# Storing and reloading kept blocks in halves, with later reload positions, in a two-channel convolution pipeline

## The reference

```python
def _L0_conv_ref(x, weight):              # per channel, 6 x 11 taps
    causal_mask = jnp.tril(jnp.ones((H, W), dtype=bool))
    xm = jnp.where(causal_mask, x, 0)
    y = conv_general_dilated(xm, weight, strides 1, feature_group_count=C)
    return jnp.where(causal_mask, y, 0)

def _L1_conv_ref(qk_dots, W1, b1, W2, b2, W3, b3):
    table = relu(relu(pos @ W1 + b1) @ W2 + b2) @ W3 + b3
    bias = table[i - j + (n - 1)]         # one value per diagonal and channel
    return qk_dots + bias

x = x + _L0_conv_ref(_gn(x), L0_conv_weight)      # _gn: mean and variance of a channel pair
x = x + _L1_conv_ref(_gn(x), ...)
```

## Time and profile before

| | us |
|---|---|
| median of 3 runs | 2928.14 |
| lowest and highest | 2927.49, 2932.59 |
| the profiled execution | 2927.91 |
| its span in the profile | 2926.2 |

### The profile page before, as it was taken

How to read it: one execution, slowest core, us unless ns; L and a number is a source line. 1 busy time by engine, 2 the same in 40 slices (tenths; PEclk the granted TensorE clock), 3 DMA queues, 4 the chain that set the end, 5 groups by cost and what they waited for, 6 DMA issues and landing times.

```text
span 2926.2 us, 81475 instructions
## 1 busy us (share of the span) xinstructions
PE 2044.5 (70%) x28880; PEld 1944.5 (66%) x28880; DVE 2305.1 (79%) x4167; ACT 1674.6 (57%) x3051; POOL 1158.7 (40%) x1988
## 2 busy tenths in 40 slices
PE   4098887876677776777768876787767778888600
PEld 0098877776677776777657776776767777787500
DVE  6788888788778888789788887878987886767624
ACT  2066665656466665666456565575656666676621
POOL 1033234534335343543345344353434534454433
PEclk9999998999788898999889897899989998899855
DMA  8885749998699987989789997999889895878798
GB/s 260 293 303 164 285 149 382 364 328 329 241 367 350 367 323 293 376 326 358 277 334 363 326 345 252 367 363 358 311 315 370 332 349 197 311 255 295 280 342 331
DMA packets 316269, 916.61 MB, mean 313 GB/s; under 512 B 39280, under 2 KB 39280, under 8 KB 313936
## 3 DMA queue, kind: packets, MB, share of 16 engines
q1 hardware_dynamic: 201952, 595.03, 56.9%
q10 hardware_dynamic: 114048, 318.80, 28.7%
HBM read 594.18 MB, written 319.68 MB: 312 GB/s over the span
## 4 chain that ended last, share of the span: by engine, by line
DMA 38%; DVE 26%; issue 15%; PE 8%; ACT 6%; POOL 2%; SPq 2%; ACTq 1%; DVEq 0%; POOLq 0%
DMA ubuf<-in_x 11%; DMA out<-kept_c_band 9%; DVE entries L724 9%; DMA out<-ubuf 7%; PE psY L1036 6%; DVE kept_c_band L863 4%; DVE XT L696 4%; DMA ubuf<-out 4%; DMA abuf<-in_x 3%; DVE psY L709 3%; DMA kept_c_band<-in_x 3%; DVE kept_c_band L711 2%; ACT junk L582 2%; PE psT L1022 2%; ACT XT L560 2%
## 5 line engine op out<-in xcount | busy, mean ns | idle before, releaser
L1036 PEld LDWEIGHTS psY<-wsplit,XT 128*128 128x128 f16 x25920 | 1658.2, 103 | 291.7 <-DVE band L711 87.1
L1036 PE MATMUL psY<-wsplit,XT 128*128 128x168 f16 (+5 forms) x25920 | 1680.7, 226 | 233.7 <-DVE kept_c_band L711 98.8
L696 DVE TENSOR_TENSOR XT<-psT,XT 128x512 f16<-128x512 f32 x720 | 491.8, 683 | 372.4 <-ACT XT L560 370.5
L1022 PE MATMUL psT<-ident,xn 128*128 128x128 f32 x2880 | 500.9, 301 | 355.3 <-POOL xn L940 261.1
L560 ACT CAST XT<-psT 128x512 f16<-128x512 f32 x720 | 414.1, 575 | 455.6 <-PE psT L1022 260.1
L971 POOL TENSOR_TENSOR ubuf<-ubuf,bias 128x1024 f32<-128x1024 f32 x184 | 415.4, 2258 | 573.4 <-ACT ubuf L602 572.5
L724 DVE BATCH_NORM_STATS2 entries<-abuf 128x6 f32<-128x512 f32 x928 | 589.5, 682 | 62.4 <-DMA abuf<-in_x 61.3
L940 POOL TENSOR_TENSOR xn<-xn,mask 128x512 f32<-128x512 f32 x336 | 422.8, 1258 | 517.7 <-ACT xn L545 439.5
L1022 PEld LDWEIGHTS psT<-ident,xn 128*128 128x128 f32 x2880 | 331.6, 151 | 369.4 <-POOL xn L940 263.5
L545 ACT ACTIVATE xn<-kept_c_band,normp 128x512 f32<-128x512 f32 (+2 forms) x496 | 398.5, 803 | 109.3 <-DMA kept_c_band<-in_x 75.8
L963 POOL COPY halo<-XT 128x16 f16<-128x16 f16 x720 | 209.8, 291 | 634.1 <-DVE XT L696 619.3
(11 more groups left out here) (76 smaller groups left out, 445.0 us busy)
## 6 DMA issues: line engine op xcount, KB each, us to landing
abuf<-in_x SPq DMA_DIRECT2D x464, 512.0 KB, 7.3
out<-ubuf ACTq DMA_DIRECT2D x288, 512.0 KB, 6.4
kept_c_band<-in_x SPq DMA_DIRECT2D x112, 1024.0 KB, 7.8
out<-kept_c_band ACTq DMA_DIRECT2D x112, 1024.0 KB, 7.8
ubuf<-in_x SPq DMA_DIRECT2D x192, 512.0 KB, 6.3
band<-in_x SPq DMA_DIRECT2D x48, 1024.0 KB, 9.7
out<-band ACTq DMA_DIRECT2D x48, 1024.0 KB, 7.9
ubuf<-out SPq DMA_DIRECT2D x96, 512.0 KB, 6.6
```

The costliest lines, as they stand in the source:

```text
L696: nc.vector.tensor_tensor(XT[:, n % NB3, 1, :, 2:P + 2], psT[n % NB3][:, :, :], XT[:, n % NB3, 0, :, 2:P + 2], ALU.subtract).then_inc(lo_r ...
L1022: last = nc.tensor.transpose(psT[m][:, i, :], xn[:, m, i, :, :].rearrange("p k c -> p (k c)"), ident[:, :])
L1036: last = nc.tensor.matmul(psY[m][:, 0:rows, o + lo_c:o + hi_c], XT[:, m, xp, i, 2 - sh:2 - sh + P], wsplit[:, c, wp, K * sh:K * sh + rows, ...
```

## The change

Each kept unit is stored and reloaded in two halves of 512 KB. The store of a half stands one position after that half's finish. The reload of half h stands at `kept_pos[blk][h] + 5`, but not later than four positions ahead of the `norm` that uses it and not earlier than `kept_pos[blk][h] + 3`. On SP the reloads stand behind the position's transit, taps and `ubuf` loads. `norm` waits for both halves. The planner books the store from the first half's position and the reload from the new one, so `ubuf` and `abuf` units move.

```diff
-    KEPT_RELOAD = 3
+    def reload_pos(blk, h):
+
+        return max(kept_pos[blk][h] + 3, min(kept_pos[blk][h] + 5, first_use(blk) - AHEAD - 4))
...
             if do_c:
-                book(kept_pos[blk][1] + 1, 1.0)
+                book(kept_pos[blk][0] + 1, 1.0)
             if do_b:
-                book(kept_pos[blk][1] + KEPT_RELOAD, 1.0)
+                book(reload_pos(blk, 0), 1.0)
...
-        kept_stored = {u: sem("kept_stored_%d%d%d%d%d%d" % u) for u in KEPT}
+        kept_stored = {(u, h): sem("kept_stored_%d%d%d%d%d%d" % u + f"_{h}") for u in KEPT for h in range(2)}
...
                         load_transit(gb, 1, n)
-                        for blk in KEPT:
-                            if kept_pos[blk][1] + KEPT_RELOAD == n:
-                                c, b = blk[:2]
-                                wait_alone(sp, kept_stored[blk], 16 * gb)
-                                sp.dma_start(part(kept[(c, b)], blk), part(xv[chan(gb, c), b], blk)
-                                             ).then_inc(kept_loaded[blk], 16)
...
-                    if do_b and n == NEXT_BIAS_LOAD:
-                        load_bias(gb, 0)
+                    if do_b:
+                        for blk in KEPT:
+                            for h in range(2):
+                                if reload_pos(blk, h) == n:
+                                    load_kept(gb, blk, h)
+                        if n == NEXT_BIAS_LOAD:
+                            load_bias(gb, 0)
+
+            def load_kept(g, blk, h):
+                c, b = blk[:2]
+                half = blk[5] // 2
+                wait_alone(sp, kept_stored[(blk, h)], 16 * g)
+                sp.dma_start(part(kept[(c, b)], blk, half * h, half), part(xv[chan(g, c), b], blk, half * h, half)
+                             ).then_inc(kept_loaded[blk], 16)
...
-                                act.wait_ge(kept_loaded[blk], 16 * (g + 1))
+                                act.wait_ge(kept_loaded[blk], 32 * (g + 1))
...
-            def store_kept(g, blk):
+            def store_kept(g, blk, h):
                 c, b = blk[:2]
+                half = blk[5] // 2
                 i = KEPT.index(blk)
-                act.wait_ge(kept_done, NR * g + 2 * i + 2)
-                act.dma_start(part(ov[chan(g, c), b], blk), part(kept[(c, b)], blk)).then_inc(kept_stored[blk], 16)
+                act.wait_ge(kept_done, NR * g + 2 * i + h + 1)
+                act.dma_start(part(ov[chan(g, c), b], blk, half * h, half), part(kept[(c, b)], blk, half * h, half)
+                              ).then_inc(kept_stored[(blk, h)], 16)
...
                         for blk in KEPT:
-                            if kept_pos[blk][1] + 1 == n:
-                                store_kept(gc, blk)
+                            for h in range(2):
+                                if kept_pos[blk][h] + 1 == n:
+                                    store_kept(gc, blk, h)
```

More of the change, by code:

```diff
@@ L664, in _ @@
             stages(act, stage)
-            for blk in KEPT:
-                act.wait_ge(kept_stored[blk], 16 * G)
+            for half_stored in kept_stored.values():
+                act.wait_ge(half_stored, 16 * G)
             for i in range(NUB):
```

## The result

The changed kernel takes 2884.16 us (median of 4 runs, 2876.63 to 2890.38) against 2927.81 us (4 runs, 2923.30 to 2932.59). The ratio is 0.985, 95% interval 0.9821 to 0.9878: a gain of 44 us, where 23 us was forecast. The profiled execution of the changed kernel took 2876.63 us and is the fastest of the four, so its profile shows 8 us more gain than the median.

The account below looks back on a forecast made before the run. No engine is full overall; DMA engines are full in most of a lap, with short holes from SP's waits for kept stores. Sum: 2927.91 - 16 - 6 - 4 + 3 = 2904.9, forecast 2905 us, range 2873 to 2937.

Parts of the forecast that it names:

- The hole at positions 24 to 27: First dip in DMA use, six laps: about 1 MB moved into it saves 2.7 us each, 16 us; bounds 0 and 19.1.
- the premise that all full stretches are a need for bytes: Where DMA engines are full, a byte moved changes nothing; only bytes moved into holes save time.
- The hole at position 52: Second DMA dip, five of six windows at 0.81 to 0.82: two thirds filled, 6 us; bounds 0 and 9.4.
- ACT's wait for `ubuf`: Stalls of 7.97 and 6.10 us should go; no time counted beyond the holes, since DMA engines are full there.
- The first rival: Full stretches are bursts, not need, so ACT's stalls are real time: 63 us less, about 2861; chance 0.12.
- The sign set for it: A gain of more than 10 us per lap would say the full stretches were not need but bursts.
- the three terms: Gains of 16 us (first hole), 6 us (position 52) and 4 us (last lap with a reload).
- The last lap with a reload: The 294 us lap, DMA share 0.75: an ACT stall counts by itself, 4 us; bounds 0 and 16.
- The start of the lap and the halves: First unit's second half lands about where the whole did: 0 counted; bounds a 10 us gain and the same loss.
- What is added: 112 more stores, each holding ACT 0.38 us, mostly in slack: 3 us charged; bounds 0 and 20.
- an estimate of 56 us per lap: By the skill's page, 2 us at each of 14 stores and 14 reloads per group; left out of the sum.
- The late half at `norm`: Rival: some reloads start later and `norm` waits for both halves; 2957, or 2930 to 2935 if half comes; chance 0.18.

Follow-up runs that it names:

- old bookings: Changed kernel with the planner's bookings of the kernel before, so ubuf and abuf units stand where they stood: 2861.98 us (0.9766), again 2857.87 us (0.9763).
- 15 MB less per lap: abuf loads bring half of each row: kernel before 2829.22 us (0.9655), changed kernel 2793.02 us (0.9523).
- The kernel with whole units: Changed kernel with one store and one reload of 1024 KB per unit, at the second half's positions: 2910.11 us, ratio 0.9931.
- Halves alone: Kernel before with stores and reloads in halves; reload positions, order on SP and bookings as before: 2880.98 us, ratio 0.9853.
- half reloads alone: Kernel before with whole stores and reloads in halves, each waiting for the whole store: 2929.30 us, ratio 1.0012.
- stores alone in halves: Kernel before with stores in halves and a whole reload that waits for both: 2924.67 us, ratio 0.9986.
- the second profile of the changed kernel: Changed kernel as it is, run again beside the one with old bookings on one chip: 2881.98 us, ratio 0.9834.

## Why the prediction was right, point by point

The sign and the range held (2884 in 2873 to 2937). The size was half of what came, and the reasoning behind the sum was right in less than that; that the time still lay in the range is in part luck, as the last point but one says.

*The hole at positions 24 to 27* (16 us). It filled as forecast, to 1.03 in all six laps, but no time came off there: positions 20 to 39 took 68.2 us before, 68.3 after and 69.4 with old bookings, where the hole is filled as well. (Within them the changed kernel was 1.4 us shorter at 30 to 34 and 2.5 longer at 35 to 39.) That filling it is worth its empty DMA time was a step that failed, and with it the premise that all full stretches are a need for bytes: 15 MB less per lap saved 6 to 14 us, not 39. The kernel with whole units has the hole filled too and is 24 to 28 us slower than the changed one.

*The hole at position 52* (6 us). It filled as well: where five windows stood at 0.81 and 0.82, six stand at 0.99 to 1.04. Positions 50 to 54 took 16.4 us after and 14.8 before.

*ACT's wait for `ubuf`* (no time beyond the holes). The stalls went, as forecast, and the step that priced them at nothing, since the DMA engines are full around them, is the one that failed most plainly: the ten positions around them took 8.7 us less per lap, 52 us in six laps. The first rival (bursts, not need) had this, mechanism and place, and priced it at 63 us. (Its sum comes to 2865; 2861 takes in the 4 us of the last lap, which it doesn't say.) The sign set for it, more than 10 us per lap, did not show, because positions 70 to 79 gave back 5 us per lap: the laps were 13, 2, 6, 5, 6 and 5 us shorter. And at positions 5 to 9 and 30 to 34 fewer bytes did make the tiles faster, so the rival is not the whole truth either.

*Positions and order on SP* were the heart of the argument. Under old bookings they are worth 26 us (0.9853 to 0.9763), close to the 26 us that the three terms gave together. The number fits by chance; the way to it is the stall at positions 15 to 19 and not empty DMA time.

*The last lap with a reload* (4 us, bounds 0 and 16). It gained 17. Here the premise was the right one, a wait counts by itself, and the term was mis-sized: it took half of one wait, where ACT's waits for DMAs fell by 16.8 us. Halves alone bring 13 us there (294 to 281), 6 of them at `norm` (its wait for the reload went from 8.8 to 2.6 us), for which the term had nothing.

*The start of the lap and the halves* (0). The wait of `norm` at the lap's start is unchanged in the changed kernel, so far right. But the step concluded from 6.4 against 7.8 us that the second half lands about where the whole one did, and stopped there. It priced each side of the split, which is worth nothing, as measured, and not the handover between them, which is worth 43 us. This is the largest miss. Nor was there a term for the end of the program, where 170 us became 164. It was 164 with halves alone, but also 165 with half reloads alone, which stores whole units at the end, so the cause is open.

*What is added.* 3 us for 112 more stores; stores alone in halves measured 0.9986, so no cost can be seen. The 1 MiB rule of the Trainium skill's page DMA: Bandwidth & Descriptors (Bandwidth) would have spoken against the split; the runs with half transfers on one side are unchanged within 0.4%, and with both sides in halves the kernel is faster. The fixed cost of 2.0 us, from which the prediction worked out an estimate of 56 us per lap, stands there (Anatomy of one DMA) for DMAs issued by GpSimd; here SP and ACT issue them, and the runs show none of it.

*The bookings.* The prediction had no term for them. The moved units were described and taken as a help for ACT's stalls only. That help is there at positions 55 to 59, 21.0 us with old bookings and 17.7 with new ones, but in all they cost about 40 us alone and 21 us in the changed kernel. Two misses of opposite sign, +21 and -43, made the sum look better than it was.

*The late half at `norm`.* The total did not grow: 75.8 us of such waits in 15 places before, 78.3 in 15 after, by the waits of the two profiles. But halves alone had brought it to 48.1, and with later positions and order it is 63.6 (old bookings), so part of what this rival feared is there, hidden by the halves.

## What to carry to other kernels

When a place in SBUF is stored and then refilled, try to hand it over in pieces: split the store and the refill together, since either alone gave nothing here. A DMA share of 0.9 in a lap, or of 1.0 in a stretch, is not proof of a bandwidth limit; take bytes away and look which stretches get shorter. A transfer that stands in a stream behind a wait it has no part in is worth moving, also where the DMA engines look full. And a planner that spreads loads by megabytes also moves the compute that belongs to them: when its inputs change, look at what lands beside what on the compute engines, and measure the move by itself.

## What the runs showed of the hardware

Splitting all 112 stores or all 112 reloads cost nothing that could be measured (0.9986 and 1.0012): transfers of 512 KB took 6.4 to 6.9 us (medians) from issue to landing in these two runs where 1024 KB took 7.8 to 8.1, with other transfers in flight. In the changed kernel the halves took 7.2 and 8.7 us, so the size says little of the time to landing. The DMA engines moved 414 to 419 GB/s in the six windows of 11 us, loads and stores mixed, most of them transfers of 512 KB. DVE's `ubuf` instruction (line 882) took 1.79 us at 1028.56 in the second profile of the changed kernel and 1.28 us at 1018.46 with old bookings for the same shape. A halo copy of POOL that ran beside the slow one took 1.20 us, where the others around it took 0.20. What slows the two was not tried.
